# Transposed activations 64 bytes further on in the on-chip memory

## What is computed

```python
x = x + 0.5 * ffn0(layernorm(x))     # 512 -> 512 with 8 LoRA experts, top 2
x = x + attention(layernorm(x))      # 32 heads of 16, 8 key heads, causal
x = x + 0.5 * ffn0(layernorm(x))
x = x + 0.5 * swiglu(layernorm(x))   # 512 -> 2 x 1376 -> 512
x = x + mamba2(layernorm(x))         # 512 -> 18560 -> ... 8192 -> 512
x = x + 0.5 * swiglu(layernorm(x))
```

## The kernel before

| tensor | address before | past a multiple of 512 |
|---|---|---|
| xTh, xTl | 32,896 and 49,280 | 128 |
| cst (constants, holds the identity) | 65,664 | 128 |
| chp (parameters) | 69,568 | 448 |
| work | 71,712 | 32 |
| wAh, wAl, wBh, wBl, wqh, wql, woh, wol | 75,968 and on | 192 |
| yTh, yTl, hh, hl, oTh, oTl, xc, eb, xdt, bT, cT | | 192 |
| w0h / w0l | 128,448 / 138,816 | 448 / 64 |
| kBD0 / kBD1 (keys of attention) | 179,296 / 75,968 | 96 / 192 |

## Time and profile before

### The profile page before, as it was taken

How to read it: one execution, slowest core, us unless ns; L and a number is a source line. 1 busy time by engine, 2 the same in 40 slices (tenths; PEclk the granted TensorE clock), 3 DMA queues, 4 the chain that set the end, 5 groups by cost and what they waited for, 6 DMA issues and landing times.

```text
span 2161.0 us, 34868 instructions
## 1 busy us (share of the span) xinstructions
PE 2116.5 (98%) x12628; PEld 1736.7 (80%) x12628; DVE 1635.2 (76%) x2661; ACT 1432.2 (66%) x3090; POOL 1052.9 (49%) x758
## 2 busy tenths in 40 slices
PE   8999999999899999999999999999999999999999
PEld 7866698887788888888888888888888888877887
DVE  7777772326888898898898888889889888896221
ACT  5598653336877777687677777768767777773332
POOL 5577555441454365345455436534545444554442
PEclk9999999999999999999999999999999999999999
DMA  3000023332333224233233322423223332231332
GB/s 137 1 2 1 1 69 93 93 88 91 114 127 137 89 88 147 87 113 114 89 107 119 137 88 89 147 88 122 104 88 116 115 132 88 95 112 54 93 94 82
DMA packets 65337, 202.53 MB, mean 94 GB/s; under 512 B 7056, under 2 KB 9104, under 8 KB 56976
## 3 DMA queue, kind: packets, MB, share of 16 engines
q1 hardware_dynamic: 65168, 200.31, 27.2%
HBM read 197.39 MB, written 2.88 MB: 93 GB/s over the span
## 4 chain that ended last, share of the span: by engine, by line
PE 92%; ACT 3%; DVE 3%; issue 1%; DMA 0%; POOL 0%; DVEq 0%; SPq 0%; ACTq 0%
PE ps L1806 87%; PE ps L2200 2%; PE ps L1991 2%; PE ps L1821 1%; ACT eb L958 0%; DVE eb L1558 0%; ACT pr_a L825 0%; ACT xTh L686 0%; DVE xTl L1207 0%; DVE bst L1184 0%; DMA w0raw<-w_in 0%; DVE PT L1414 0%; DVE rs L1359 0%; ACT pr_b L825 0%; ACT eb L965 0%
## 5 line engine op out<-in xcount | busy, mean ns | idle before, releaser
L579 POOL TENSOR_TENSOR wAl<-rawA,wAh 128x512 fp32r<-128x512 f32 x233 | 339.9, 1472 | 377.3 <-ACT wAh L719 376.7
L1806 PE MATMUL ps<-xTh,wAh 128*128 128x512 f32 (+1 forms) x1520 | 425.3, 401 | 5.8 <-DVE xTl L1207 3.1
L1806 PE MATMUL ps<-xTl,wAh 128*128 128x512 f32 (+1 forms) x1520 | 415.0, 394 | 0.0
L1806 PE MATMUL ps<-xTh,wAl 128*128 128x512 f32 (+1 forms) x1520 | 414.6, 394 | 0.0
L1512 DVE SCALAR_TENSOR_TENSOR work<-ps,chp,work 128x510 f32<-128x510 f32 (+2 forms) x465 | 344.1, 744 | 31.2 <-ACT work L921 21.2
L1806 PEld LDWEIGHTS ps<-xTl,wAh 128*128 128x128 f32 x1520 | 284.8, 188 | 69.1
L1806 PEld LDWEIGHTS ps<-xTh,wAl 128*128 128x128 f32 x1520 | 284.7, 188 | 69.1
L1806 PEld LDWEIGHTS ps<-xTh,wAh 128*128 128x128 f32 x1520 | 276.0, 188 | 74.4 <-issue 12.7
L585 POOL TENSOR_TENSOR wBl<-rawB,wBh 128x512 fp32r<-128x512 f32 x108 | 139.4, 1304 | 392.1 <-ACT wBh L723 392.1
L958 ACT ACTIVATE eb<-eb,gc 128x128 f32<-128x128 f32 x1008 | 307.5, 391 | 0.0
L921 ACT ACTIVATE work<-ps,gpar 128x512 f32<-128x512 f32 x155 | 119.4, 770 | 140.2 <-PE ps L1806 107.8
(11 more groups left out here) (210 smaller groups left out, 3966.8 us busy)
## 6 DMA issues: line engine op xcount, KB each, us to landing
eb<-scr_decays SPq DMA_DIRECT2D x62, 1536.0 KB, 6.5
rawA<-ma_in SPq DMA_DIRECT2D x144, 256.0 KB, 6.8
rawA<-fa_in SPq DMA_DIRECT2D x88, 256.0 KB, 2.6
rawB<-mb_in SPq DMA_DIRECT2D x64, 256.0 KB, 2.8
rawB<-fb_in SPq DMA_DIRECT2D x44, 256.0 KB, 2.6
x<-x_in SPq DMA_DIRECT2D x8, 256.0 KB, 6.1
x_out<-x SPq DMA_DIRECT2D x8, 256.0 KB, 2.7
wqraw<-wqkv_in SPq DMA_DIRECT2D x1, 1536.0 KB, 10.1
```

What stands on the lines that cost most here:

```text
L579: nc.gpsimd.tensor_tensor(wAl[:, slot, :], rawA[:, slot, :], wAh[:, slot, :].bitcast(F32), ALU.subtract).then_inc(A_lo, 1)
L1806: return nc.tensor.matmul(o, l, r, start=start, stop=end, **kw)
```

## The change

One tensor, `bst` (48 bytes in use, 64 taken; per-tile layer norm statistics), is placed ahead of xTh and not behind `work`:

```diff
     x = place("x", [P, NT, D], F32)
+    bst = place("bst", [P, 2, 6], F32)
     xTh = place("xTh", [P, KC, NT * P], F32R)
     xTl = place("xTl", [P, KC, NT * P], F32R)
     cst = place("cst", [P, C_END], F32)
     chp = place("chp", [P, CP_END], F32)
     work = place("work", [P, 2, D], F32)
-    bst = place("bst", [P, 2, 6], F32)
     bmv = place("bmv", [P, 2, 2], F32)
```

## The result

The changed kernel takes 2141.99 us, the median of four runs (2141.35 to 2142.84), against 2161.83 before: 19.8 us less, a ratio of 0.9907 with a 95% interval of 0.9895 to 0.9919. Forecast were 2135.2 us, so 26.6 us less, in a range of 2127 to 2152. The profiled execution took 2141.35 us with a span of 2139.6 (before 2162.77 and 2161.0), 21.4 us less.

A forecast was written before the change was run, and what follows sets the result against it. TensorE's matmul pace was taken to bound the kernel; -30.1 us for pace, +5.0 for run-in and -1.5 for neighbours gave -26.6 us, so 2135.2 us from 2161.83, own range 2131 to 2139, wider range 2127 to 2152.

The forecast's parts named there:

- rival B: Input-projection stretches between breaks never settle and stay at 230.9 ns a matmul: 10.8 us less, 2151.0 us; chance 0.12.
- The pace: Input, gate/up and dt products: 4512 matmuls with 512 columns go from 233.3 to 226.7 ns, 30.1 us less.
- The run-in: Input projection chunks behind a break start slower: 112 times 45 ns, so 5.0 us of the gain are not had.
- The neighbours: Output and down projections stop inheriting the slower pace of the matmuls before them: 0.6 and 0.9 us, together 1.5 us less.
- Expert, q/k/v and first pair: Expert and q/k/v products, 576 matmuls whose stationary operand moves: 3.9 us either way, taken as zero.
- What is late next: VectorE's decays in a Mamba2 step: 0.75 us of slack less 0.32 us leaves 0.4 us, so no wait appears.
- The sum: Whole kernel: -30.1 + 5.0 - 1.5 = -26.6 us, span 2134.4 us, median 2135.2 us; chance 0.68.
- A: The address distance isn't the cause: the input projection stays at 233.3 ns and the time at 2161.8 us; chance 0.12.
- C: Equal distances make weight load and stream collide: input projection at 240 ns, 30.1 us more, 2191.9 us; chance 0.05.
- D: The input projection's stream falls to 220 ns a matmul: 60 us less, 2102 us; chance 0.03.

The follow-up runs named there:

- experiment 3: A separate kernel without the computation: streams of 36 float32r matmuls at sixteen differences between moving-operand and weight addresses; 226.7 to 234.3 ns a matmul.
- experiment 6: Changed kernel again: 2145.43 us; with GpSimd held until the decays in second steps: 2138.73 us; with those decays held until GpSimd's subtraction: 2146.84 us.
- experiment 1: Kernel of before with the weights, not the activations, moved 448 bytes, so both start 128 past a multiple of 512; 2138.95 us, ratio 0.9897.
- experiment 7: Changed kernel with GpSimd held until the decays in every step but the very first: 2135.89 us; second steps only: 2137.64 us; changed kernel alone: 2141.12 us.
- experiment 2: Changed kernel with 64 free bytes ahead of the weights, restoring the difference of minus 64 bytes; 2162.48 us, ratio 1.000.

## Why the prediction was right, and where it was off

**The time.** The measured median, 2141.99 us, is 6.8 us over the forecast 2135.2 and outside the 2131 to 2139 that went with it; only the wider range, drawn out to rival B, holds it. The pace is right to a tenth of a nanosecond; what is off is a wait that the sum put at nothing, and the clock, which it left out.

**The pace: right.** 226.7 ns was taken for 4512 matmuls from the rows at equal distance and was measured. The mean of all starts between 200 and 300 ns apart is 227.40 ns in the input projection, 233.37 before; 4512 times the difference is 26.9 us, run-in included, where the sum had 30.1 - 5.0 = 25.1. The table of experiment 3 says why the reasoning held: the rows compared two of its columns. What I added to it, that 13.3 ns is the usual cost and minus 64 an exception, was wrong. I had mixed widths: the q/k/v and expert products have 384 and 324 columns, where the difference hardly counts.

**The run-in: right in kind, too large.** 5.0 us were kept for it, 45 ns at 112 breaks. The 227.40 lies 0.73 ns over 226.7, which is 3.3 us over all 4512.

**The neighbours: right.** Forecast 1.5 us. Output projection 228.03 to 227.77 ns and down projection 228.55 to 227.20 ns in the same mean give 0.4 + 0.7 = 1.1 us.

**Expert, q/k/v and first pair: right to take as zero.** q/k/v, now at difference 0, went from 173.3 to 174.0 ns, the experts from 149.3 to 149.0, and the 48 matmuls with 256 columns cost 0.2 us more, the last 16 at 119.4 ns where the earlier trace rows had 113.1.

**"What is late next": this step failed.** I took the slack of one step, 0.75 us, subtracted the 0.32 us by which TensorE gains on it, and said that no wait appears. Two things were wrong.

The slack was that of the wrong step, measured to the wrong instruction. In the step of the earlier trace rows TensorE needs the first decay at 1046.76 and the second one only at 1048.12:

```profile
1048.12 0.61 PE L1806 MATMUL ps<-eb,xdt 128*64 128x128 f32 x8
```

The first is over at 1044.87, so its slack is 1.9 us, and the second's is 2.1. The closest cover is in the second step of a group, 0.70 us to the first decay (experiment 6), a step that the rows don't show. That 0.75 is so near to 0.70 is luck: two errors cancelled. So is the remainder of 0.4 us, which is what these steps have after the change where VectorE wins, 0.43 us.

And the remainder was compared with nothing. The decays of the earlier trace rows are as long as when VectorE wins, but the lengths in the trace before reach from 1.2 to 2.3 us:

```profile
L1558 DVE TENSOR_TENSOR eb<-eb,cbD x128: 1206/1215/2305, 542.4 to 1937.5; 128x1024 f32<-128x1024 f32 x128
```

A slack of 0.4 us has to be compared with the longest of them, 1.1 us more than the usual one. The price is 0.88 us a group (177.95 for 177.07), of it 0.7 us at the decays and the rest mostly at the later wait for VectorE's sums; three times in the first profile, 2.6 us, and seven times in the second, some 6. The sign that I had named for being wrong, TensorE waiting for the decays and giving the gain back there, came true for that part of it.

**The sum.** It forecast 2134.4 us for the span. Without lost collisions in the second steps it was 2135.2 and 2135.8 (experiments 1 and 6), so 0.8 and 1.4 us over it. The 2139.6 us of the first profile lie 5.2 us over it: half of that are the late decays, and most of the rest are the clock at the end of the Mamba2 stage and the later start (experiment 7).

**The rivals.** A fell with experiments 1 and 2, B with the settled rows. C is not what happens at 512 columns, but it is at 256, where equal distances cost 6.7 ns more. D didn't happen: at 512 columns no difference went under 226.7. The Trainium skill's rule in "SBUF — State Buffer", section "Who interferes with whom", that the two reads of TensorE are independent agrees with what bfloat16 does here (215.8 ns at three differences) and not with float32r (226.7 to 234.3 ns).

## What to carry to other kernels

When TensorE is the bound, measure the distance from start to start per kind of matmul, and where two kinds of one shape differ, compare the layout before anything else; for float32r with 512 columns put moving operand and weights at the same distance from a multiple of 256 bytes, and try it anew for each width. After TensorE has become faster, compare every slack that is left with the longest duration of what it covers, not with the usual one. Where two engines start within 0.1 us of one another and hold each other up, the time varies from run to run: make one wait where it has time. And before a spread is put down to such a collision, look at the granted clock of the runs.

## What was not expected of the hardware

- The pace of float32r matmuls with 512 columns depends on the difference of the operands' addresses with a period of 256 bytes (in the sixteen steps of 32 bytes tried), from 226.7 to 234.3 ns; bfloat16 takes 215.8 and plain float32 429.2 ns at each of three differences.
- With 256 columns the order turns round: 120.0 ns at difference 0, 113.3 at minus 64.
- With 128 and with 192 columns a float32r matmul with its weight load takes the same time, 111.7 ns.
- After the change the same two instructions start 0.07 to 0.08 us apart in 21 steps of three profiles of one kernel; VectorE was held up in 14 of them and GpSimd in 7.
- The unchanged kernel's runs lie within 2.3 us (2161.01 to 2163.26), those of the changed one between 2137.8 and 2149.5 us. Lost collisions are one part of that, up to 6 us in a profile; the granted clock, 0.995 to 0.998 over these runs, goes with another.
